# Cross-attention kernel: how many score matmuls stand in each quarter of a step, and where the softmax denominators stand

## The reference

```
x = x + attention(layernorm(x), ctx, ctx)      # 32 query heads, 8 key/value heads of 32 columns, softmax over 512 keys
x = x + ffn(layernorm(x), ...)                 # a gate picks one of 8 small adapters for each row
```

## Time and profile before

| what | value |
|---|---|
| median of three runs | 1094.2 us |
| profiled execution, device time | 1095.06 us |
| profiled execution, span of the trace | 1093.2 us |
| busy: PE, DVE, POOL, ACT | 970.6, 919.3, 774.0, 756.3 us |
| mean granted TensorE clock | 0.996 of full speed |

### The profile page before, as it was taken

How to read it: one execution, slowest core, us unless ns; L and a number is a source line. 1 busy time by engine, 2 the same in 40 slices (tenths; PEclk the granted TensorE clock), 3 DMA queues, 4 the chain that set the end, 5 groups by cost and what they waited for, 6 DMA issues and landing times.

```text
span 1093.2 us, 18664 instructions
## 1 busy us (share of the span) xinstructions
PE 970.6 (89%) x6442; PEld 337.3 (31%) x6442; DVE 919.3 (84%) x1202; ACT 756.3 (69%) x1333; POOL 774.0 (71%) x373
## 2 busy tenths in 40 slices
PE   3269999999999999999999999999999998999994
PEld 2112222222222222222222222222222225776771
DVE  4669999999999899889999999988888874889964
ACT  5348878888788888778878878877767666544430
POOL 2017888888888888888888888888988897111100
PEclk9999999999999999999999999999999999999998
DMA  7744767576767676766666666756455643755322
GB/s 200 203 109 97 163 135 178 136 175 137 172 136 166 133 163 138 165 138 160 143 160 146 164 145 157 156 117 149 105 125 139 154 100 110 248 197 206 139 115 116
DMA packets 324545, 163.88 MB, mean 150 GB/s; under 512 B 187229, under 2 KB 312157, under 8 KB 324453
## 3 DMA queue, kind: packets, MB, share of 16 engines
q1 hardware_dynamic: 324452, 162.70, 60.7%
HBM read 107.84 MB, written 54.53 MB: 149 GB/s over the span
## 4 chain that ended last, share of the span: by engine, by line
PE 45%; DVE 35%; issue 15%; ACT 3%; DMA 1%; POOL 0%; SPq 0%; DVEq 0%; ACTq 0%; POOLq 0%
DVE row_max L809 22%; PE psum L500 10%; PE psum L476 9%; PE psum L488 9%; PE psum L439 5%; PE psum L592 5%; DVE o_t L815 4%; PE psum L573 3%; DVE probs L1004 3%; PE psum L465 2%; DVE prod_mem L868 2%; PE psum L562 1%; DVE stats L837 1%; DMA k_split<-k_parts 1%; DVE k_parts L862 1%
## 5 line engine op out<-in xcount | busy, mean ns | idle before, releaser
L729 ACT ACTIVATE probs<-psum 128x512 f32<-128x512 f32 x1024 | 553.5, 595 | 161.3 <-PE psum L476 156.1
L809 DVE TENSOR_REDUCE row_max<-psum 128x4 f32<-128x2048 f32 x256 | 584.2, 2282 | 39.0 <-PE psum L439 30.5
L280 POOL TENSOR_TENSOR sums<-probs 128x2048 f32<-128x2048 f32 x64 | 290.9, 4546 | 56.6 <-ACT probs L729 56.6
L476 PE MATMUL psum<-q_stack,k_stack 97*128 97x512 f16 x1024 | 317.9, 386 | 12.5 <-ACT probs L729 10.2
L292 POOL TENSOR_TENSOR sums<-probs 128x2048 f32<-128x2048 f32 x64 | 291.6, 4556 | 26.0 <-ACT probs L729 26.0
L488 PE MATMUL psum<-probs,v_in 128*32 128x512 f32 x2048 | 273.6, 606 | 5.1 <-ACT probs L729 2.6
L476 PEld LDWEIGHTS psum<-q_stack,k_stack 97*128 97x128 f16 x1024 | 78.3, 97 | 254.0 <-ACT probs L729 147.0
L439 PE MATMUL psum<-high_mem 32*128 32x512 f16 x1024 | 103.1, 391 | 39.3 <-DVE row_max L809 28.3
L500 PE MATMUL psum<-sums,ones 128*32 128x512 f32 x1024 | 121.6, 592 | 0.0
L821 DVE STREAM_TRANSPOSE den_t<-psum 128x512 f32<-128x512 f32 x64 | 45.9, 717 | 64.7 <-PE psum L500 64.7
L256 POOL TENSOR_TENSOR o_t<-o_t,inv 128x512 f32<-128x512 f32 x64 | 67.2, 1049 | 37.5 <-DVE inv L827 37.5
(11 more groups left out here) (93 smaller groups left out, 703.1 us busy)
## 6 DMA issues: line engine op xcount, KB each, us to landing
q_stack<-q_split SPq DMA_DIRECT2D x192, 128.0 KB, 3.3
xa<-in_x_dram SPq DMA_DIRECT2D x32, 512.0 KB, 3.6
q_split<-prod_mem SPq DMA_DIRECT2D x16, 1024.0 KB, 5.6
o_all<-in_x_dram SPq DMA_DIRECT2D x256, 64.0 KB, 2.3
x_attended<-o_all SPq DMA_DIRECT2D x64, 256.0 KB, 4.4
out_dram<-probs SPq DMA_DIRECT2D x32, 512.0 KB, 2.9
high_mem<-q_split SPq DMA_DIRECT2D x64, 128.0 KB
high_mem<-k_split SPq DMA_DIRECT2D x64, 128.0 KB
```

Source lines behind the costliest of these rows:

```text
L280: pool.tensor_tensor(sums[:, (2 * u - 1) % SUMS], probs[:, (u - 1) % 2, 2], probs[:, (u - 1) % 2, 3], ALU.add).then_inc(back_done, 1)
L476: pe.matmul(st_ps[:, bank_of["score", u, n], :], k_stack[:, u % SLOTS, t * P:(t + 1) * P], q_stack[:, u % SLOTS, g, :], start=True, stop=T ...
L729: act.activation(probs[:, s, t, g, :], st_ps[:, bank_of["score", u, n], :], ACT.Exp, scale=EXP_SCALE).then_inc(exped, 1)
L809: dve.reduce_max(row_max[:, u % 2, t:G * ST:ST], s_ps[:], AX.X).then_inc(reduced, 1)
```

## The change

Sixteen scores stay sixteen and every other operation stays too; only places change. The scores of a step stand 5, 5, 3, 3 in its quarters instead of 4, 4, 4, 4. The first two of a quarter stand ahead of the gather as before; the other 3, 3, 1, 1 stand behind it. The denominators of the unit before leave their place behind the gather of quarter 3. In odd steps all of them stand right behind the `score_rows` of quarter 3. In even steps the first half stands at the end of quarter 2, ahead of those `score_rows`, and the second half right behind them. ScalarE's other work follows the new numbers: `high_part` of quarter 1 comes behind exponential 4, that of quarter 2 behind exponential 9, and the centring pass stands ahead of exponential 13, not 14. VectorE's and GpSimd's orders stay. The planner gets the new order.

```diff
+            BEGIN = (0, 5, 10, 13, NSC)
+            MIDST = (2, 7, 12, 15)
...
-                    scores = [("score", u, t * G + g) for g in range(G)] if live(u) else []
+                    scores = [("score", u, n) for n in range(BEGIN[t], BEGIN[t + 1])] if live(u) else []
+                    half = MIDST[t] - BEGIN[t]
...
-                    filled += scores[:2]
-                    if t == ST - 1 and live(u - 1):
-                        filled.append(("den", u - 1, 0))
+                    filled += scores[:half]
                     if t == 2 and live(u + 1):
                         filled.append(("max", u + 1, 0))
-                    filled += scores[2:]
+                    filled += scores[half:]
+                    if t == 2 and live(u - 1):
+                        filled.append(("den", u - 1, 0))
...
-                def denominators(u):
+                def first_denominators(u):
                     wait(pe, front_done, u + 1)
-                    wait(pe, back_done, u + 1)
                     bank_free("den", u, 0)
                     wait(pe, den_taken, u)
...
+                def last_denominators(u):
+                    wait(pe, back_done, u + 1)
...
+                        if t == ST - 1 and live(u - 1) and live(u):
+                            if u % 2 == 1:
+                                first_denominators(u - 1)
+                            last_denominators(u - 1)
                         if u % 2 == 1 and t < PIECES and whole(tile_of(u)):
                             turn_part(tile_of(u), t)
                         if live(u):
-                            score_keys(u, t, 0)
+                            score_keys(u, BEGIN[t], MIDST[t])
...
-                        if t == ST - 1 and live(u - 1) and live(u):
-                            denominators(u - 1)
                         if t == 2 and live(u + 1):
                             turn_max(u + 1)
                         if live(u):
-                            score_keys(u, t, 1)
+                            score_keys(u, MIDST[t], BEGIN[t + 1])
+                        if t == 2 and live(u - 1) and live(u) and u % 2 == 0:
+                            first_denominators(u - 1)
```

More of the change, by code:

```diff
@@ L466, in turn_part, with score_keys @@
                     last.then_inc(turned, 1)
-                def score_keys(u, t, pair):
-                    if t == 0 and pair == 0:
+                def score_keys(u, begin, end):
+                    if begin == 0:
                         wait(pe, s_in[u % SLOTS], 96 * (u // SLOTS + 1))
                         wait(pe, shift_in[u % 2], 16 * (u // 2 + 1))
-                    for g in (2 * pair, 2 * pair + 1):
-                        n = t * G + g
+                    for n in range(begin, end):
+                        t, g = n // G, n % G
                         bank_free("score", u, n)
@@ L490, in gather @@
                     last.then_inc(pv_done, 1)
-                def denominators(u):
+                def first_denominators(u):
                     wait(pe, front_done, u + 1)
-                    wait(pe, back_done, u + 1)
                     bank_free("den", u, 0)
                     wait(pe, den_taken, u)
[L498 to L501, removed]
+                    for g in range(G):
+                        pe.matmul(st_ps[g * D:(g + 1) * D, bank_of["den", u, 0], :], ones[:, 0:D],
+                                  sums[:, 2 * u % SUMS, g, :], start=True, stop=False)
+                def last_denominators(u):
+                    wait(pe, back_done, u + 1)
+                    for g in range(G):
+                        last = pe.matmul(st_ps[g * D:(g + 1) * D, bank_of["den", u, 0], :], ones[:, 0:D],
+                                         sums[:, (2 * u + 1) % SUMS, g, :], start=False, stop=True)
                     last.then_inc(den_done, 1)
@@ L603, in body @@
                         project(q, 1)
-                        denominators(UNITS - 1)
+                        first_denominators(UNITS - 1)
+                        last_denominators(UNITS - 1)
                     if before:
@@ L719, in _ @@
                             s = u % 2
[L720 to L724, removed]
+                            for n in range(BEGIN[t], BEGIN[t + 1]):
+                                keys, g = n // G, n % G
+                                if g == 0:
+                                    wait(act, pv_done, ST * (u - 2) + keys + 1)
+                                    wait(act, front_done if keys < ST // 2 else back_done, u - 1)
+                                if n == MIDST[2] and live(u + 1):
                                     make_shift(u + 1)
-                                if t == ST - 1 and g == G // 2:
+                                if n == BEGIN[ST - 1]:
                                     centring_pass()
                                 wait(act, scored, NSC * u + n + 1)
-                                act.activation(probs[:, s, t, g, :], st_ps[:, bank_of["score", u, n], :], ACT.Exp,
+                                act.activation(probs[:, s, keys, g, :], st_ps[:, bank_of["score", u, n], :], ACT.Exp,
                                                scale=EXP_SCALE).then_inc(exped, 1)
```

## The result

The changed kernel takes 1118.76 us (median, 1118.01 to 1121.01), for 1094.18 before: a ratio of 1.022, 95% interval 1.0203 to 1.0236. It is slower, as forecast, but by 24.6 us and not by 6, and 0.8 us beyond the upper end of the range. Its profiled execution took 1118.38 us with a span of 1116.6.

What follows compares the result with a forecast made beforehand. Bound: VectorE's maximum needs four row scores and the next row scores need that maximum; quarter 3 by TensorE. Terms +12.5, +0.5 and -7.3 make +5.7 us, on 1094.2 forecast as 1100, range 1077 to 1118.

Steps and rivals of the forecast that it cites:

- the sum: Whole kernel: +12.5 us over 25 pairs of steps, +0.5 for step 1, -7.3 for twelve late steps, in all +5.7.
- odd steps with parts: a loss of 0.98: Odd steps holding parts: bank waits on TensorE lengthen each from 13.78 to 14.76 us, with quarters 2 and 3 returning 0.71.
- three waits: Odd steps, TensorE: part 0 waits for denominators (0.5), score 4 for `low_part` (0.3), part 1 for exponential 4 (0.73).
- Even steps: a gain of 0.48: Even steps 2 to 50: halved denominators shorten each from 12.66 us by 0.48; bounds nothing and 0.74.
- Late steps: a gain of 0.6: Steps 52 to 63, no parts: even ones gain 0.83, odd ones 0.40 on 12.75 us, twelve steps -7.3.
- Step 1 +0.5: Start of the loop: step 1 loses 0.5 us, as its part 0 does not wait for denominators.
- the upper bound of the odd steps (+1.69): Odd steps with parts: a loss of 1.69 us each if the last two quarters give nothing back.
- The narrower range: The forecast's own range: odd steps +0.8 to +1.2, even ones -0.6 to -0.3, total 1093 to 1112.
- Odd steps did not hide their waits: First rival: odd steps hide their waits, 13.3 us each, total 1062, chance 0.12; half the loss gone, 1081, chance 0.16.
- The second rival: Even and late gains fail as half denominators delay each maximum: +25 us, 1119, chance 0.16.
- The clock did not fall in the loop: Third rival: clock falls in quarter 1 of odd steps, 3.15 us of TensorE work at half speed, +82, 1182, chance 0.02.
- The rule of the Trainium skill on cycling through PSUM banks: Bank cycling with small idles can make the clock fall and rise; the forecast took this to cost nothing here.

Runs made afterwards that it cites:

- e3: Changed kernel, planner's counts 7 for a part and 6 for the denominators, plus one wait ahead of the feed-forward part: 1108.0 us, ratio 1.0108.
- e7: As e6, but all denominators stand at the head of quarter 3 in odd steps with parts too, scores there still 4, 4, 4, 4: 1101.9 us, ratio 1.0066.
- e12: Changed kernel; steps 0, 1 and odd steps with parts in old form, planner counts denominators 4, parts 8, denominators halved in all late steps: 1091.8 us, ratio 0.9976.
- e11: Kernel before, only the planner puts score 3 of odd steps with parts into the parts' bank: 1117.34 us, ratio 1.0214.
- e8: As e7, but the denominators stand in halves on both sides of the last row scores in odd steps too: 1112.7 us, ratio 1.0163.
- e1: Changed kernel, only the planner's count of places for a part is 8 instead of 6: 1123.2 us, ratio 1.0247.
- e6: Changed kernel, odd steps with parts keep old distribution and denominators' place; planner's count for denominators 5 instead of 3: 1092.1 us, ratio 0.9976.
- e10: Changed kernel, only the SyncE queue differs: the next unit's shift goes ahead of the store of the split parts: 1165.1 us, ratio 1.0643.

## Why the prediction was wrong, point by point

**The step that failed is the sum, in the sizes of its terms.** It forecast +5.7 us and the span grew by 23.4. All five rows of the table above came out above their forecast: the odd steps by 8.1 us, the start by 3.3, the even steps by 2.6, the late ones by 2.5, the end by 1.2. The largest is the term "odd steps with parts: a loss of 0.98", which measured 1.30.

- **Direction: right. Mechanism: in the trace, but only a part of the loss.** The bank of part 0 taken by score 4, with three waits behind it, is there, and the same bank use put alone into the kernel before costs 0.92 per odd step. Yet with those waits gone (e3) the odd step still takes 0.73 more than before, of 1.21. Of this rest, quarters 0 and 1 take 1.46 more than before, with scores 4 and 9 waiting 0.47 and 0.38 for exponentials, and quarters 2 and 3 give back 0.73. That it is the five scores on two banks is read from these waits; no run takes it apart from the new place of the denominators, which in e7 costs 0.16 in a step of 4, 4, 4, 4. The forecast had counted this chain on ScalarE, but named only the three waits as the cause, and had not put the five scores as a cost of their own.
- **"Odd steps with parts: a loss of 0.98": too small.** Regular odd steps lose 1.21, all of them 1.30. A part starts 0.15 us behind the end of the instruction that frees its bank, where 0.05 to 0.08 had been taken: part 0 at 605.15, behind a transpose that ends at 605.00, and part 1 at 609.07, behind an exponential that ends at 608.92 (4.15 from the first maximum, forecast 4.01). The second maximum was still nearly where it was forecast (3.43 for 3.39), the third came at 8.05 for 7.79. Quarter 3 was 4.04 for 3.97. The irregular 0.09 was not foreseen.
- **"Even steps: a gain of 0.48": nearly right**, 0.41 in regular steps, 0.37 in the mean, since step 2 alone takes 13.16. Half the denominators cost 1.0, not 0.92, and a score alone 0.32, not 0.27. The maxima came at 2.84, 5.75 and 9.05, where the forecast's own times give 2.83, 5.61 (row scores at 5.17, and 0.44) and 8.87; so the half ahead of the last row scores costs 0.49, not 0.31.
- **"Late steps: a gain of 0.6": too large.** They take 12.23 and 12.59, a gain of 0.34 on 12.75. In the even ones it is the same two durations; in the odd ones the third maximum comes at 5.76 for 5.61 and quarter 3 takes 4.04 for 3.96. For the odd ones e12 shows what was missed: with the halves split there too they take 12.23.
- **"Step 1 +0.5": the step that failed most for its size.** Steps 0 and 1 cost 3.7 (the first 0.1 lies ahead of step 0). I had taken the durations of the steady loop for all steps, and put step 0 at nothing. Step 1 lost 1.95: what every odd step loses, and a wait that the forecast denies ("in steps 1 and 3 only part 0's predecessor is another"). In step 1 score 14 too has the bank of denominators:

```profile
97.56 0.39 PE L480 MATMUL psum<-q_stack,k_stack 97*128 97x512 f16 x1 [0.85 <-DVE den_t L836]
```

Step 0 lost 1.75. In its first part every matmul takes about twice its later time, in both kernels, and when that ends differs from run to run. The trace's first record of the granted clock marks the moment:

| run | scores in step 0 | first clock record, us | step 0 |
|---|---|---|---|
| e11 | 4, 4, 4, 4 | 74.69 | 12.77 |
| kernel before | 4, 4, 4, 4 | 76.75 | 13.34 |
| e12 | 4, 4, 4, 4 | 77.42 | 13.34 |
| e8 | 5, 5, 3, 3 | 74.74 | 13.74 |
| e1 | 5, 5, 3, 3 | 75.03 | 13.88 |
| e6 | 5, 5, 3, 3 | 77.26 | 14.32 |
| changed kernel | 5, 5, 3, 3 | 80.00 | 15.09 |
| e3 | 5, 5, 3, 3 | 82.40 | 15.65 |

At like moments the new distribution costs about 1.0 here (an estimate, from 13.74 less 12.77 and 14.32 less 13.34); the other 0.75 or so came with the later moment (15.09 less 14.32). e1 and the changed kernel issue the same matmuls in the same order within 0.1 us of each other up to 73.4 us, and yet the moments are 5 us apart; no run shows what sets them. Where steps 0 and 1 keep their old form (e12) 2.9 us are gone, and the earlier moment has its part in that.
- **The end: 1.2 us** behind the last denominators, not forecast, with the same instructions: the granted clock, as shown above. It isn't a cost of the change.
- **The range** reached 1118. Its terms were bounded each, but the upper bound of the odd steps (+1.69) was not carried into it: the 25 x 1.30 that was measured is +32.6 by itself. The gains were taken as certain together with the loss. The narrower range in it is also off: odd steps +0.8 to +1.2 and even ones -0.6 to -0.3, with the other terms as they stand, give 1092 to 1110 and not 1093 to 1112.
- **Rivals.** Odd steps did not hide their waits. The second rival's number, 1119, is the measured one, but by luck: its mechanism is that the even and late steps gain nothing, and they gained 14 us. The clock did not fall in the loop: the granted clock is 1.00 from 99 to 783 us, at 2.4 GHz, with TensorE idle 47 us of 684 there (36 of 661 before). The rule of the Trainium skill on cycling through PSUM banks, as quoted ahead, does not show itself in this trace either. That holds for waits of up to 1.0 us as the change makes them; behind the longer ones of e10 the clock did fall.

```profile
99.00:783.00 684.00, 636.74 (x4300) 163.59 (x4299) 596.20 (x545) 525.52 (x974) 580.42 (x224) 1.00 0.64 143
```

## What to carry to other kernels

When an order of matmuls is changed, write down for each use of a rotating bank which use it follows, before and after; the balance of the engines in each quarter says little if a score now sits between two uses that a slower engine has to read. A greedy planner's counts are part of the order: the same even steps took 12.25 to 13.32 us under different neighbours. One edit that brings a loss of the right size into the old kernel doesn't show that the same cause makes all of it in the new one; take the cause out of the new one too. And price the first iterations from their own rows, not from the steady ones.

## What the runs showed of the hardware

In step 0 a window's granted clock reads 1.00, and yet the matmuls are at half their later speed. The eight matmuls of a gather in the changed kernel, in step 0 and one quarter 3 later:

```profile
73.37 1.94 PE L492 MATMUL psum<-probs,v_in 128*32 128x512 f32 x8
...
81.55 1.07 PE L492 MATMUL psum<-probs,v_in 128*32 128x512 f32 x8
```

TensorE had waited 2.40 us for VectorE ahead of 68.18, and did its full-speed work from about 80 us. The trace has no record of the clock ahead of 80.00 us (76.75 in the kernel before), and the windows count such time as 1.00. In all fourteen traces the last slow score starts less than 3 us ahead of that first record, and the first fast one behind it. So ahead of the first record the number 1.00 says nothing; the mean time of one instruction does.

A busy time can grow with no instruction added: TensorE's went up by 16 us, 12 of them in steps 2 to 51, while the mean length of a score's record stayed (386 ns before, 387 after). The records of matmuls overlap. Two scores in a row are busy for 0.60 us, two apart for 0.39 each. The new order has more places where matmuls stand apart; how much of the 16 us that is was not measured by itself.
